# A two-layer local-attention network on one Trainium2 core: where VectorE's Newton step and ScalarE's root of the variances stand in the pipeline's step

## The reference, cut to what matters

```python
h = shift_token(x)                      # second half of the channels from the token before
q, k, v = split(h @ wqkv)               # 8 heads of 64
q = l2norm(q) * qs;  k = l2norm(k) * ks
q, k = rotary_xpos(q, k)
o = local_attention(q, k, v)            # windows of 128 tokens, each sees itself and the one before
x = x + o @ wo
h = shift_token(x)
h = (h - mean(h)) / sqrt(var(h) + 1e-5) * lg + lb
a, g = split(h @ w1 + b1)
x = x + (a * gelu(g)) @ w2 + b2
```

## Time and profile before

| | |
|---|---|
| median of three runs | 5481.87 us |
| the profiled execution, its own time | 5489.2 us |
| its span, first to last instruction | 5487.4 us |
| mean granted TensorE clock | 0.871 |
| busy: TensorE, VectorE, ScalarE, GpSimd | 81%, 60%, 47%, 34% |
| the two layers | about 1690 us to the end |

### The profile page before, as it was taken

One profiled execution on the slowest core, in us unless ns is written; L12 is line 12 of the kernel. 1 busy time (PEld: TensorE's weight loads), 2 busy tenths in 40 slices (PEclk: granted clock), 3 DMA queues, 4 the chain that ended last, 5 costly groups with the idle time before them and its releaser, 6 DMA issues. The chain is left out here.

```text
span 5487.4 us, 99781 instructions
## 1 busy us (share of the span) xinstructions
PE 4421.5 (81%) x33294; PEld 3182.8 (58%) x33294; DVE 3304.6 (60%) x7541; ACT 2602.7 (47%) x5522; POOL 1868.5 (34%) x1466
## 2 busy tenths in 40 slices
PE   4889888888985887888878888677878788787886
PEld 2444444444434666666666666556666666666665
DVE  5566666666636565755657556465656557575564
ACT  1444444544444554545545455354545445454453
POOL 3021323122113433433334333234444344343443
PEclk6788888988867998999989999888989889899998
DMA  5332442443202000000000000010000000000000
GB/s 128 71 91 49 95 102 41 99 100 94 44 20 66 14 13 13 11 13 14 13 13 11 13 14 13 15 58 21 16 20 17 16 22 15 20 15 18 17 17 19
DMA packets 148566, 200.28 MB, mean 36 GB/s; under 512 B 21708, under 2 KB 122536, under 8 KB 148016
## 3 DMA queue, kind: packets, MB, share of 16 engines
q1 hardware_dynamic: 143920, 192.13, 14.5%
q10 hardware_dynamic: 4096, 1.06, 0.1%
HBM read 116.02 MB, written 67.68 MB: 33 GB/s over the span
## 5 line engine op out<-in xcount | busy, mean ns | idle before, releaser
L1580 POOL TENSOR_TENSOR b_e<-b_e,b_share 128x512 f32<-128x512 f32 (+1 forms) x512 | 534.9, 1045 | 1284.8 <-DVE b_share L2010 1284.8
L1032 DVE TENSOR_REDUCE a_mx<-a_ring 128x2 f32<-128x1024 f32 (+3 forms) x768 | 726.3, 956 | 388.4 <-PE a_ring L851 190.1
L698 ACT ACTIVATE a_e_t<-a_ring 128x1024 f32<-128x1024 f32 (+3 forms) x768 | 614.1, 811 | 698.8 <-PE a_ring L851 441.9
L1681 ACT ACTIVATE b_e<-b_e,b_bias 128x256 f32<-128x256 f32 (+1 forms) x1024 | 501.0, 491 | 614.5 <-DVE b_bias L1990 613.5
L1786 PE MATMUL b_bank_m<-b_h_t_hi,b_w_hi 128*128 128x256 f32 x1584 | 476.4, 301 | 96.6 <-issue 72.5
L1786 PE MATMUL b_bank_p<-b_wqkv_hi,b_turned_hi 128*128 128x512 f32 x768 | 372.6, 485 | 183.5 <-ACT b_qk L1653 137.8
L1786 PE MATMUL b_bank_m<-b_h_t_lo,b_w_hi 128*128 128x256 f32 x1584 | 462.2, 292 | 0.0
L1786 PE MATMUL b_bank_m<-b_h_t_hi,b_w_lo 128*128 128x256 f32 x1584 | 461.4, 291 | 0.0
L864 PE MATMUL a_ring<-a_k_st,a_q_st 48*128 48x512 f32 (+3 forms) x1536 | 367.4, 476 | 101.6 <-ACT a_e_t L698 73.5
L889 PE MATMUL a_ring<-a_q_st,a_k_st 50*128 50x512 f32 (+3 forms) x1536 | 381.9, 496 | 79.5 <-DVE a_qk_p L1011 40.3
L2086 DVE SCALAR_TENSOR_TENSOR b_ag<-b_bank_m,b_b_c,b_ag 128x256 f32<-128x256 f32 x396 | 191.4, 483 | 403.0 <-ACT b_ag L1709 397.5
(11 more groups left out here) (229 smaller groups left out, 11061.7 us busy)
## 6 DMA issues: line engine op xcount, KB each, us to landing
a_q_st<-a_parts_q SPq DMA_DIRECT2D x192, 128.0 KB, 4.6
a_k_st<-a_parts_k SPq DMA_DIRECT2D x192, 128.0 KB, 7.5
b_fl<-f_rows SPq DMA_DIRECT2D x72, 256.0 KB, 4.0
a_parts_q<-a_qk_p SPq DMA_DIRECT2D x16, 1024.0 KB, 9.1
a_parts_k<-a_qk_p SPq DMA_DIRECT2D x16, 1024.0 KB, 5.1
a_xl<-in_L_attn_x SPq DMA_DIRECT2D x9, 1024.0 KB, 9.1
f_rows<-b_fr SPq DMA_DIRECT2D x33, 256.0 KB, 2.1
b_x_l<-x_rows SPq DMA_DIRECT2D x33, 256.0 KB, 3.0
```

Of the source, the lines that this page charges most:

```text
L698: act.activation(e_t[:, step % 2, 2 * pair:2 * pair + 2, 0:cols], slot[:, :].rearrange("p (h t) -> p h t", h=2)[:, :, 0:cols], ACT.Exp).th ...
L1032: dve.reduce_max(mx[:, g % 2, :, pair, piece, t:t + 1], slot[:, :].rearrange("p (r c) -> p r c", r=2)[:, :, 0:cols], AX.X)\
L1580: pool.tensor_tensor(weights, weights, share[:, pp, :].unsqueeze(2) .broadcast_to([P, 2, 2 * WIN - lo]), ALU.mult).then_inc(e_done.sem, 1)
L1681: ins = act.activation(weights, weights, ACT.Exp, scale=-1.0, bias=bias[:, pp, hh:hh + 1], accum_out=total[:, pp, hh:hh + 1])
```

## The change

On VectorE, `inverse_norms` moves from behind the row tops and the MLP's first products to the front of its step, ahead of the wait for the scores and of `shares`. On ScalarE, the piece `moments` (the root of the variances) is left out of its step and done at the end of the next one, behind that step's other pieces.

```diff
@@ ScalarE
                     for x in pieces_at(pp, closing):
-                        piece_of_mlp(*x)
+                        if x[0] != "moments":
+                            piece_of_mlp(*x)
+                    for piece, u, m in pieces_at(pp - 1, closing):
+                        if piece == "moments":
+                            piece_of_mlp(piece, u, m)
@@ VectorE
+                        if pp % PAIRS == 1 and (pp + 3) // PAIRS < NWIN:
+                            inverse_norms((pp + 3) // PAIRS)
                         if 0 <= pp < NPP:
                             scores_met(pp)
                         if 0 <= pp - 1 < NPP:
...
                         else:
                             activated(pp, 0, 3)
-                        if pp % PAIRS == 1 and (pp + 3) // PAIRS < NWIN:
-                            inverse_norms((pp + 3) // PAIRS)
                     activated(pp, 3, HK)
```

## The result

| | before | after |
|---|---|---|
| median, same chip | 5482.49 us | 5655.99 us |
| lowest to highest of 4 | 5463.68 to 5487.91 | 5629.65 to 5671.85 |
| the profiled execution, its own time | 5489.2 | 5629.65 |
| busy VectorE | 3304.6 us | 3025.3 us |
| mean granted TensorE clock | 0.871 | 0.88 |

The ratio is 1.0318, 95% interval 1.0266 to 1.0370: 173 us slower, where 150 were forecast against the median. VectorE does the same work in 279 us less busy time, and the kernel is slower by 3%.

What follows compares the result with a forecast made beforehand. The prediction took a closed ring across GpSimd, TensorE and VectorE as the bound. Terms 77 + 56 + 24 - 6 = +151 us on 5489 gave 5640, or 5632 us for the median; the 8-in-10 range was 5565 to 5700 us.

Steps and rivals of the forecast that it cites:

- a closed ring: Share, `share_out`, rotation, q transpose, scores, row tops, products, next share: no slack at VectorE's share; grows 1.02 us per window.
- Newton in steps 5, 17 and 25: Newton step ahead of the share there: share, `share_out`, rotation and q transpose each come 1.02 us later.
- Newton in step 9: Newton step ahead of step 9's share: share, `share_out`, rotation and q transpose come 1.02 us later.
- Newton in step 1: Hidden by GpSimd's gate products in the second layer, partly in the first; 0.3 us taken, ends 0 and 1.02.
- step -3: No share here, but the Newton step meets GpSimd's rotation ahead of the first `ag` product; 0.4 us, ends 0 and 2.5.
- unit -1's root: At a sample's start `norm` comes 3.5 us later with nothing covering it; 56 us, bounds 3.0 and 4.5 a sample.
- unit 2's root: Steps 29 to 31: the share and all behind it down to `ag` move 1.5 us later; 24 us, bounds 0 and 1.8.
- units 0 and 1: Steps 13 to 15 and 21 to 23: k projection fills a stall; -0.2 us each, -6 us, between -1.0 and +0.5.
- the clock, slower still: Rival: new waits in steps 10 and 18 bring half clock on TensorE; +50 to +100 us, 5680 to 5735; chance 0.10.
- Steps 13 and 21: Newton step hidden behind the transfer of shifted rows; cost 0, 1.02 us without this cover, old 3.41 us's saving worth nothing.
- VectorE paces, faster: Rival: VectorE's saved 2.39 us a window, or ScalarE's 238.6 us, lies in the ring; 5428 us; chance 0.06.
- Absorbed: Rival: unseen slack and the sample's start held by its loads leave some 10 us; 5470 to 5505 us; chance 0.04.

Runs made afterwards that it cites:

- step 9 alone: The kernel before with the Newton step at the front of its step in step 9 only; 5491.61 us, ratio 1.0004.
- the Newton step alone: The kernel before with only VectorE's edit, ScalarE's root left in its old place; 5581.82 us, ratio 1.0151.
- a run of its own: The kernel before with the root moved for units 0 and 1 and the Newton step at the front in steps 13 and 21 only; 5463.17 us, 0.9960.
- The root alone: The kernel before with only ScalarE's edit, the Newton step left in its old place; 5555.57 us, ratio 1.0108.
- the filled wait: The changed kernel with eight spare TensorE transposes ahead of the wait for the rotation in step 10; 5651.96 us, ratio 1.0301.

## Why the prediction was right, and where its terms were off

The mechanism was right: a closed ring with the share in it, and a start with nothing to cover a later `norm`. The sum came closer than its terms. Here they stand beside the stretches of after, in us of the whole program:

| term | forecast | after, from the table |
|---|---|---|
| Newton in steps 5, 17 and 25 | 49 | 45 |
| Newton in step 9 | 16 | 42 |
| Newton in step 1 | 5 | 4 |
| start up to the first scores: Newton in step -3, unit -1's root | 62 | 73 |
| unit 2's root, steps 28 to 32 | 24 | 21 |
| units 0 and 1, steps 12 to 16 and 20 to 24 | -6 | -22 |
| sum (151 in the prediction's own rounding) | 150 | 163 |

- **The ring and its price: right.** Steps 5, 17 and 25 were priced at 1.02 us each and grew by 1.09, 1.07 and 0.66 us. The run with step 9 alone grew by 1.11.
- **Step 9: mis-sized.** It grew by 2.61 us against 1.02. The cause is the one that the prediction gave to its rival "the clock, slower still": a low stretch behind the two waits of step 10, in a window that had none. The rival expected it in steps 10 and 18 at 1.6 to 3.2 us. It came in step 10 alone, at 1.5 us, 24 us in all; the window of step 17 kept a granted clock of 1.00. As a mechanism it belonged in the sum, and as a case it did not come: the time stays short of 5680 us.
- **Step -3: too low.** 0.4 us was taken, since TensorE is two fills ahead. With the Newton step alone the first scores of a pass come 61.75 us behind the share of step 32 instead of 60.40, so 1.35 us later. In that run's timeline its L157 takes 1.20 us beside the rotation, against 0.17.
- **Step 1: right.** From the first scores to the share of step 1 the same run takes 1.49 us more, and steps 1 to 4 take 1.48 less; in after it is 1.51 and 1.05. The net is 0.0 to 0.5 us, and 0.3 was taken.
- **Steps 13 and 21: cost 0 is right** where the root is moved too, as it is in after; a run of its own shows it. "Their saving is worth nothing either" is not: with the root in its old place the Newton edit shortened these stretches by 0.86 and 0.77 us (granted clock 0.901 to 0.964 in the first). Which of its places did that was not taken apart.
- **The start's root: right.** 3.56 us against 3.5, with the Newton step in place, in 14 passes and not 16: 50 us instead of 56.
- **Unit 2's root: the place right, but it reaches further.** Steps 28 to 32 grew by 1.29 us (1.5 forecast). The root alone costs 5.58 us in the start, which no term had. Its trace divides this: unit -1's variances come 1.62 us later behind the share of step 32 (33.95 against 32.33 us), which is mostly what unit 2 leaves behind (the move for units 0 and 1 alone gives 0.28 of it), and `norm` comes another 4.08 us later, within the bounds for unit -1. With unit -1's root in its old place most of the first part is hidden: the start is 69.14 us with the other units moved and 68.84 with the Newton step alone.
- **Units 0 and 1: the sign right, the size too small.** -0.48 and -0.87 us in after against -0.2 each, and the root's move for them by itself gains 28 us. The prediction weighed the end of the stall (VectorE late next, which is right) and gave nothing for the clock behind it, though the row that it quoted had the 0.80 us in it.
- **The upper end of the range.** 5680 us is called a bound, but no sum is given for it. All upper bounds of the terms together make 5738 us.
- **"VectorE paces, faster" is out.** VectorE lost 279 us of busy time and the program became 173 us longer.
- **"Absorbed" is out**: the plain windows and the start both grew.

The sum came out near 173 partly by luck. Step 9 and the start were taken 37 us too low and the other terms 24 us too high, and the 6 us between the layers had no term.

By the Trainium skill, page "SBUF — State Buffer", section "SBUF: two separate sides", an operation of VectorE in a two-port mode, or one with two SBUF inputs against one of GpSimd that reads SBUF, shares an exclusive lock with GpSimd's: whichever starts first has it for the whole instruction, and the other fully blocks. The traces agree: 0.18 us ahead of the share, 1.04 to 1.19 behind it, and GpSimd loses too (1.97 against 1.04). The section says what an operation takes and not who waits for it; taken as the rule for the whole change, as in the first rival, it pointed the wrong way.

## What to carry to other kernels

Before moving a slow operation to where it runs fast, find who waits for what it now stands in front of: 1.1 us ahead of a signal in a closed ring cost more than 3.4 us behind it. Look for the ring across engines, for both its arms, and take out of it what nobody waits for. And test a move of several places place by place: of the six kinds of place in this change one was a gain (the root of units 0 and 1), one was free (the Newton step in steps 13 and 21), and four were losses (the Newton step in the plain windows and in steps -3 and 1, the root of unit -1 and of unit 2).

## What the runs showed of the hardware

- In 15 of 16 passes of after, TensorE's clock fell to the lower level behind two waits, of 1.16 to 1.42 and of 0.82 to 0.84 us, with 4.00 of 4 us busy just ahead in the pass shown. In the fifth pass of the same execution, and in all 16 of the kernel with step 9 alone, it stayed at 1.00 behind waits of 1.16 to 1.18 and 0.83 to 0.84 us with the same work around them. What tells them apart stays open.
- When one window changed, the low stretches moved in others. 1.1 us added to a window (step 9 alone) or 1.4 us taken from one (the filled wait) changed the medians of the whole by 4 us, where 18 and 22 were due, and windows with no changed instruction moved by up to 0.8 us.
- A multiplication of 128x8 by a scalar (L1974) took 1.18 us beside GpSimd's rotation and 0.17 us without.
